# One TensorE product packed and one weight preparation spread over an earlier stage

## The reference

```
# layer 0's feed-forward: two layers of local attention and a gated unit, HID = 682
for l in range(2):
    h = shift_token(x); q, k, v = split(h @ wqkv); ...           # 8 heads of 64, window 128
    x = x + attention(q, k, v) @ wo
    h = layernorm(shift_token(x)) * ln_g + ln_b
    a, g = split(h @ w1 + b1)                                    # 682 units each
    x = x + (a * gelu(g)) @ w2 + b2

# layer 1's feed-forward: 8 experts, the best 2 for a token, capacity 640 tokens an expert
# layer 2's feed-forward: everything rounded to 8 bits and scaled back
scale_w = max(|w|, axis=1) / 127;   wq = clip(round(w / scale_w), -128, 127) * scale_w
scale_x = sigmoid(clip_x) * max(|x|) / 127                       # one maximum over all tokens
xq = clip(round(x / scale_x), -128, 127) * scale_x
h  = silu(xq @ wq_gate.T) * (xq @ wq_up.T)                       # 704 units
x  = x + quantised(h) @ wq_down.T                                # a maximum over all of h as well
```

## Time and profile before

| | us |
|---|---|
| median of 3 runs | 1743.97 (1742.27 to 1746.13) |
| the profiled execution's own time | 1745.38 |
| its span, first to last instruction | 1743.6 |
| TensorE busy | 1443.5 (83% of the span) |
| VectorE busy | 1057.2 (61%) |
| ScalarE busy | 736.5 (42%) |
| GpSimd busy | 450.7 (26%) |
| mean granted TensorE clock | 0.903 of 2.4 GHz |

### The profile page before, as it was taken

How to read it: one execution, slowest core, us unless ns; L and a number is a source line. 1 busy time by engine, 2 the same in 40 slices (tenths; PEclk the granted TensorE clock), 3 DMA queues, 4 the chain that set the end, 5 groups by cost and what they waited for, 6 DMA issues and landing times. The chain is left out here.

```text
span 1743.6 us, 30751 instructions
## 1 busy us (share of the span) xinstructions
PE 1443.5 (83%) x9502; PEld 1155.4 (66%) x9503; DVE 1057.2 (61%) x2850; ACT 736.5 (42%) x1768; POOL 450.7 (26%) x474
## 2 busy tenths in 40 slices
PE   4977999999999999999987983599165599629992
PEld 3764777778777777877764573488142488528992
DVE  4445776666777777777756623676887576452223
ACT  1304555555656655555643310254186144213330
POOL 4222222222212222322322074121312100046321
PEclk9978999999999999999997997799585699759996
DMA  8000000000000000000003453600100000112104
GB/s 305 1 1 1 1 2 1 0 1 0 1 26 33 2 1 0 0 0 0 2 2 143 181 175 136 250 1 0 37 1 1 4 1 0 48 49 83 46 32 150
DMA packets 27280, 74.73 MB, mean 43 GB/s; under 512 B 6602, under 2 KB 11995, under 8 KB 25146
## 3 DMA queue, kind: packets, MB, share of 16 engines
q1 hardware_dynamic: 20378, 55.57, 8.5%
q0 software_dynamic: 6816, 18.14, 3.4%
HBM read 54.35 MB, written 20.88 MB: 43 GB/s over the span
## 5 line engine op out<-in xcount | busy, mean ns | idle before, releaser
L1130 PE MATMUL banks<-l_ffn_h2T,l_ffn_in_w 128*128 128x128 f32 (+1 forms) x1536 | 193.4, 277 | 0.0
L1130 PEld LDWEIGHTS banks<-l_ffn_h2T,l_ffn_in_w 128*128 128x128 f32 (+1 forms) x1536 | 178.6, 179 | 11.1 <-issue 5.7
L1047 PE MATMUL banks<-l_ffn_in_wqkv,l_ffn_hT 128*128 128x512 f32 x384 | 182.6, 613 | 0.8 <-ACT l_ffn_hT L1207 0.8
L1229 ACT ACTIVATE l_ffn_work<-l_ffn_work,l_ffn_att_bias 128x256 f32<-128x256 f32 x256 | 126.4, 495 | 76.9 <-DVE l_ffn_att_bias L1377 76.9
L1257 ACT ACTIVATE l_ffn_gate<-banks,l_ffn_layer_cols 128x128 f32<-128x128 f32 x192 | 59.8, 362 | 201.0 <-PE banks L1130 187.8
L1047 PEld LDWEIGHTS banks<-l_ffn_in_wqkv,l_ffn_hT 128*128 128x128 f32 x384 | 69.5, 194 | 75.9 <-issue 74.8
L1138 PE MATMUL banks<-l_ffn_in_w,l_ffn_ff 128*128 128x256 f32 (+1 forms) x384 | 107.8, 396 | 0.0
L996 POOL TENSOR_TENSOR l_ffn_rden_wide<-l_ffn_att_rden,ones 128x512 f32<-128x512 f32 x32 | 33.3, 1041 | 272.1 <-DVE l_ffn_att_rden L1388 272.1
L265 POOL TENSOR_TENSOR rstd<-mean_var,neg_half 128x1 f32 x48 | 26.4, 550 | 263.8 <-DVE mean_var L258 263.8
L2191 DVE COPY l_plan_c_all<-l_ffn_in_w 128x1024 f32 x39 | 31.1, 798 | 100.6 <-PE banks L2125 88.2
L1263 ACT ACT_TABLE_LOAD x68 | 87.2, 1283 | 1.2
(11 more groups left out here) (414 smaller groups left out, 3454.4 us busy)
## 6 DMA issues: line engine op xcount, KB each, us to landing
l_plan_rows<-l_plan_pairs SPq DMA_DIRECT2D x16, 512.0 KB, 7.8
l_ffn_in_w<-in_L_w SPq DMA_DIRECT2D x2, 4096.0 KB, 20.8
l_ffn_in_down<-in_L_down SPq DMA_DIRECT2D x1, 4096.0 KB, 13.3
l_plan_pairs<-l_plan_rows SPq DMA_DIRECT2D x4, 1024.0 KB, 8.0
l_plan_table<-l_plan_rows SPq DMA_DIRECT2D x8, 512.0 KB, 2.8
l_ffn_in_wqkv<-in_L_wqkv SPq DMA_DIRECT2D x1, 3072.0 KB, 12.7
l_ffn_in_w<-in_L_w SPq DMA_DIRECT2D x2, 1364.0 KB, 14.0
x_res<-in_x SPq DMA_DIRECT2D x4, 512.0 KB, 5.5
```

The source lines that it names most:

```text
L1047: mm = pe.matmul(ps[:, (Q, K, V)[n], :], hT[:, m.b, m.odd, ch, 1 - ch:P + 1 - ch], wqkv[:, bass.ds(m.layer, 1), ch, n * INNER:(n + 1) * IN ...
L1130: mm = pe.matmul(ps[0:FW[j], HIDDEN[pair], to:to + P], w1[:, ch, at:at + FW[j]], h2T[:, ch, m.b, :], start=(j % 2, n, ch) == (0, 0, 0), st ...
L1229: ex = nc.scalar.activation(work[:, m.b, slot, :], work[:, m.b, slot, :], ACT.Exp, bias=bias[:, m.b, slot:slot + 1], scale=-1.0, accum_out ...
```

## The change

There are three edits.

**The last 42 units.** `w1` gets 640 columns of values, 640 of gates and 128 more, in which the last 42 values stand from column 0, the last 42 gates from column 64, and zeros between. The sixth chunk is then one product of 128 columns and not two of 42; its gates come out on partitions 64 to 105. `load_up` loads `w1` in four DMAs, the biases of the last gates get a copy of their own on those partitions, and GpSimd clears the columns between.

**The weights of layer 2's feed-forward.** They are loaded in `l1_xattn` and quantised in layer 1's experts, by a class `Quantiser`. VectorE takes all largest values and scales before its first copy. The rest goes in six pieces (four of the gate and up weights, two of the down weights), between the tiles: scaling at tiles 1 to 6 and rounding at tiles 4 to 9 on ScalarE, clipping at tiles 4 to 9 on VectorE, turning at tiles 11 to 16 on TensorE, copying out at tiles 12 to 17 on VectorE. The rounding is on ScalarE and no longer on GpSimd.

**What is left in layer 2's feed-forward.** One block in place of three: normalising, the maximum of `x`, its spread, the scales, GpSimd's clearing of a part of `h`, and SyncE's loads for the next attention. The last layer's router takes three of its buffers in memory that is kept longer now.

```diff
+FULL = (FCH - 1) * P
+LAST = HID - FULL
+GATES_AT = 64
+def load_up(sp, w1, of, loaded):
+    for at, first, n in ((0, 0, FULL), (FULL, HID, FULL), (2 * FULL, FULL, LAST), (2 * FULL + GATES_AT, HID + FULL, LAST)):
+        sp.dma_start(w1[:, :, at:at + n], of[..., first:first + n].rearrange("l p c n -> (l p) c n")).then_inc(loaded, 16)
...
                     for j in (2 * pair, 2 * pair + 1):
-                        for n in range(2):
-                            at, to = n * HID + j * P, (2 * (j % 2) + n) * P
+                        for n in range(1 if j == FCH - 1 else 2):
+                            at, to = n * FULL + j * P if j < FCH - 1 else 2 * FULL, (2 * (j % 2) + n) * P
                             for ch in range(DCH):
-                                mm = pe.matmul(ps[0:FW[j], HIDDEN[pair], to:to + P], w1[:, ch, at:at + FW[j]],
+                                mm = pe.matmul(ps[:, HIDDEN[pair], to:to + P], w1[:, ch, at:at + P],
...
+class Quantiser:
+    def scales(self, v, dve):
+        dve.link(v.memset(inv[:], 1.0))
+        v.wait_ge(raw.loaded, raw.all)
+        v.tensor_reduce(ffn.gu_scale[:], raw.w_gu[:], AX.X, ALU.max, apply_absolute_value=True)
+        dve.link(v.tensor_reduce(self.d_scale[:], raw.w_d[:], AX.X, ALU.max, apply_absolute_value=True))
...
+    def clip(self, v, k):
+        v.wait_ge(s.scaled.sem, s.scaled.at(k))
+        v.tensor_scalar(of, of, LOW, HIGH, ALU.max, ALU.min).then_inc(s.clipped.sem, 1)
...
@@ shared_hidden_experts
+    SCALED_FROM, CLIPPED_FROM, TURNED_FROM = 1, 4, 11
...
                 down_product(t)
+                if TURNED_FROM <= t < TURNED_FROM + PIECES:
+                    quantiser.turn(pe, t - TURNED_FROM)
...
+            quantiser.scales(v, dve)
             for t in range(n_tiles):
...
                 v.tensor_copy(flat(hT[:, t % 2, :, :]), ps[t % 3]).then_inc(s.rowT_ready.sem, 1)
+                if CLIPPED_FROM <= t < CLIPPED_FROM + PIECES:
+                    quantiser.clip(v, t - CLIPPED_FROM)
+                if TURNED_FROM + 1 <= t < TURNED_FROM + 1 + PIECES:
+                    quantiser.take(v, t - TURNED_FROM - 1)
...
@@ l2_ffn
-            with nc.Block() as block:
-                @block.tensor
-                def _(pe):
-                    for n in range(2):
-                        for ch in range(DCH):
...
+            @block.tensor
+            def _(pe):
+                turned_maximum_pe(e, pe, one[:], all_row[:], 1, 0)
...
-                dve.link(v.tensor_scalar(xs[:, 0:1], allmax[:], sig[:, 0:1], None, ALU.mult))
+                for k in range(ALL_TILES):
+                    c = v.tensor_scalar(c_all[:, k, :], e.x[:, k, :], e.mean_var[:, k, 0:1], e.rstd[:, k:k + 1], ALU.subtract, ALU.mult)
```

More of the change, by code:

```diff
@@ L226, in build @@
         with ExitStack() as later:
+            ffn = L2Ffn(e, later)
             x2 = Xattn(e, later, "L2_", True)
@@ L515, in _ @@
                 p.memset(ffn.vv[:], 0.0)
+                for at, n in ((2 * FULL + LAST, GATES_AT - LAST), (2 * FULL + GATES_AT + LAST, P - GATES_AT - LAST)):
+                    p.memset(ffn.w1[:, :, at:at + n], 0.0)
             s.prep_psum.each(1)
@@ L1982, with __init__ @@
 HIDDEN_AHEAD = DROPPING_TILES
-def shared_hidden_experts(e, ctx, stage, plan, w_down):
+QI = 704
+QCH = -(-QI // P)
+QW = [min(P, QI - j * P) for j in range(QCH)]
+QMAX = 127.0
+MAGIC = 1.5 * 2.0 ** 23
+LOW, HIGH = MAGIC - QMAX - 1.0, MAGIC + QMAX
+PIECES = 6
+GU_PIECES = 4
+class L2Ffn:
+    def __init__(self, e, ctx):
+        sb = memory(e, ctx, "l2_ffn_kept")
+        self.matrices = sb("matrices", [P, DCH * 2 * QI + QCH * D], BF16)
+        self.w_guT = self.matrices[:, 0:DCH * 2 * QI].rearrange("p (c n i) -> p c n i", c=DCH, n=2)
+        self.w_dT = self.matrices[:, DCH * 2 * QI:].rearrange("p (j d) -> p j d", j=QCH)
+        self.gu_scale = sb("gu_scale", [P, 2 * QCH])
+        self.d_row = sb("d_row", [P, D])
+        self.sig = sb("sig", [P, 2])
+        self.magic = sb("magic", [P, 1])
+        self.less_magic = sb("less_magic", [P, 1])
@@ L1988, in shared_hidden_experts @@
+def shared_hidden_experts(e, ctx, stage, plan, w_down, quantiser):
     nc, s, ps = e.nc, e.s, e.ps
@@ L2683, in l3_xattn @@
     cross_attention(e, "L3_", False, True, given)
-QI = 704
-QCH = -(-QI // P)
-QW = [min(P, QI - j * P) for j in range(QCH)]
-QMAX = 127.0
-MAGIC = 1.5 * 2.0 ** 23
-class L2Ffn(Ahead):
-    def __init__(self, e, ctx):
-        sb = memory(e, ctx, "l2_ffn_in")
-        self.w_gu = sb("w_gu", [P, 2 * QCH, D])
-        self.w_d = sb("w_d", [P, DCH, QI])
-        self.clips = sb("clips", [P, 2])
-        super().__init__(e, "l2_ffn", ((self.w_gu, "L2_gu"), (self.w_d, "L2_d"), (self.clips, "L2_clips")))
 def l2_ffn(e, ffn, *following):
```

300 lines of the change are left out of this document (163 added, 137 removed).

## The result

The changed kernel takes 1715.93 us (median of 4 runs, 1714.74 to 1717.60), the kernel before on the same chip 1745.05: a ratio of 0.9829, 95% interval 0.9816 to 0.9842. It is faster by 29 us, and the forecast was 38. The profiled execution has a span of 1712.9 us, 30.7 less than before. I cut both traces at the first instruction of each stage and at its end; the columns are us.

A forecast was written before the change was run, and what follows sets the result against it. TensorE was taken to bound layer 0's feed-forward, TensorE and GpSimd to be near their limits in layer 1's experts. -14.4 + 2.0 - 28.1 + 2.3 = -38.2 us gave 1706; own range 1700 to 1711, 8-in-10 range 1695 to 1720.

The forecast's parts named there:

- The packed product: Layer 0's feed-forward: each item 0.45 us shorter, 14.4 us gained over 32 items, ends 24 and 0.
- Rival 1: Layer 0's feed-forward: gated values come in time, each item gains all 0.76 us, kernel 1696; chance 0.12.
- rival 2: Layer 0's feed-forward: a second wait takes the rest, the packed product brings nothing, kernel 1720; chance 0.11.
- The loads at the start: Block at 17 us: four more SyncE issues of 0.51 us, 2.0 us lost, ends 1.5 and 3.
- Layer 2's feed-forward: Start of that stage: first loop 13.9 us after the first normalising, 28.1 us gained, ends 29.7 and 26.5.
- four parts: Before layer 2's first loop: normalisings 5.23, largest values 4.42, maximum, spread and scales 2.59, GpSimd's clearing 1.6 us.
- the memset's hold of VectorE: Layer 2's feed-forward: GpSimd's clearing of h beside VectorE's normalising adds 1.6 us.
- Layer 1's experts: Stage that takes in the quantising: 2.3 us lost, between 1.3 and 5.8.
- 0.5 + 3.6 - 1.8: Layer 1's experts: late first copy 0.5 us, TensorE's turning 3.6, less slack 1.8 before the last scatter.
- The slack: End of layer 1's experts: last scatter starts later than its data is there, hiding 1.8 us of delay.
- GpSimd's issues: Layer 1's experts: meetings with six VectorE clips add at most 1.2 us, hidden behind TensorE's 4.1.
- The prediction's other figure: Layer 1's experts, by the skill's lock rule: GpSimd's chain 2.6 us longer, stage ending 2.6 later in place of 2.3.

The follow-up runs named there:

- quantise only: The changed kernel with the packed product taken back, leaving the quantising in pieces alone: 1751.56 us, ratio 0.9846 to the kernel before.
- pack only: The kernel before with the packed product alone, its four loads, bias copy and cleared columns included: 1777.17 us, ratio 0.9991 to the kernel before.

## Why the prediction came out as it did

- **The packed product, right.** 0.45 us an item was forecast and (781.3 - 766.7) / 32 = 0.46 came, by the mechanism named: TensorE now comes before VectorE's gated values, and one item's down product starts 1.53 us behind the up products in place of 1.99. Rival 1 (no wait) and rival 2 (a second wait) are both out. That the stage agrees to 0.2 us is luck in part: it takes 765.6 to 769.8 us in the traces of all kernels with this edit and the same order of TensorE, and 781.3 and 783.3 in the two without it, a gain of 11.5 to 17.7.
- **The loads at the start, wrong.** This is the step "there are four issues more in it ...: 4 x 0.51 = 2.0 us lost", with 3 as the upper end. It took one issue's duration for a constant. The direction and the place were right (all on the path), the size was 10.5: two of the issues took 3 and 6 us. That they do so behind a backlog is shown by the kernel that issues the narrow loads first; what besides the backlog makes an issue stall is open. The rows of before could have warned of the backlog: ten loads are issued in 5 us there, the last lands long after, and splitting one load of 128 rows into four of 256 multiplies what stands in the queue.
- **Layer 2's feed-forward, right,** 28.3 for 28.1, with each of its four parts within 0.2 us, the memset's hold of VectorE among them.
- **Layer 1's experts, too small.** Of "0.5 + 3.6 - 1.8" the turning was right (3.66). The start was 2.2, not 0.5: a few tenths are VectorE's, the rest is the clock's moment, which no row of one trace can price: the same stage's first three distances sum to 6.95 us in quantise only and to 8.97 here. The slack was 1.0 and not 1.8, since a scatter starts 0.78 us behind its copy's end when it waits for it. GpSimd's issues, priced at up to 1.2 for the clips, came to 1.2: one clip's meeting took 1.31 us in place of 0.95, as this timeline of the changed kernel shows, and it hid behind TensorE as forecast. The prediction's other figure, 2.6 for a hold over the whole length of every clip, did not come: GpSimd's busy time in the stage went from 46.75 to 47.93 us.

```profile
1022.41 0.55 DVE L2129 TENSOR_SCALAR l_ffn_raw_w_gu<-l_ffn_raw_w_gu 128x768 f32<-128x768 f32 x1
1022.47 1.31 POOL L2190 DMA_INDIRECT l_plan_rows<-l_plan_table,l_plan_token  x1 [0.30 <-issue]
```

- **What was not in the sum.** -2.6 us in the last attention and +0.5 in layer 1's attention and router. I take the first for the clock's moment, as above; for the second no run was made. With them -38.2 + 8.5 + 2.4 - 2.6 + 0.5 = -29.4; the span shortened by 30.7, and the rest is in tenths over the other stages.

The time lay inside the stated range by luck: it is outside the forecast's own 1700 to 1711, and the wider range had been drawn for other rivals (1720 for a product that brings nothing). Its upper end was right for a wrong reason.

## What to carry to other kernels

Before splitting a load, or adding one to a block that ends with SyncE, look at what is already in the queue: an issue of 0.5 us can become one of 3 or 6 behind a backlog, on every engine that the block joins. No count of rows or loads found here says when, so the trace of the changed kernel has to. Loads that nobody waits for soon belong in a block with long work, not in the short one before it. Work that is moved into a stage should go where the stage waits for something that isn't an engine, such as the landing of its last DMAs, and with buffers enough that it doesn't form a chain of its own there.

## What the runs showed of the hardware

- A DMA issue on SyncE took 0.3 to 1.1 us in the loads at the start, but for the last two pieces of `w1` where all four end the list: there it took 2.3 to 3.2 and 6.0 to 6.1 us in all ten traces, whether their rows had 168 or 2560 bytes. In layer 1's attention two loads took 2.4 to 3.8 us each in the eleven traces with the packed product, 0.4 to 0.5 in the two without it.
- VectorE's normalising was held by GpSimd's memset: 1806 ns for an instruction of 399. The Trainium skill ("SBUF — State Buffer", section "SBUF: two separate sides") calls the port pair that both use an exclusive lock for the whole instruction. The traces agree: with ScalarE's clearing of the same size in place of the memset, all sixteen took 5.25 us together, as in the kernel before (5.23).
- TensorE's granted clock rose at different moments of a stage in different executions. The last attention, whose code is the same in all kernels, took 140.5 and 138.7 us in two executions of the changed kernel, and 136.4 to 143.1 over all kernels. At the start of layer 1's experts the clock was back at full speed 11.2 us behind the first gather in one execution of the changed kernel and 8.5 in the other.
- Two of the three chips of the experiments took some 20 us longer for layer 1's experts, pack only with its unchanged experts among them. The changed kernel's trace there has TensorE idle for 11.7 and 5.7 us at two tiles, up to VectorE's copies; why these come late isn't shown.
